# Causal stage of a four-block transformer kernel: gathering, inverting and fanning out the row sums of sixteen heads on four column groups

## What is computed

```python
dot = jnp.einsum('bhid,bhjd->bhij', q, k)                    # 16 heads of 16 features
vals = q_norm_sq + k_norm_sq.transpose(0, 1, 3, 2)
scores = dot * dot / (vals - 2.0 * dot + EPSILON)
scores = scores + mask[None, None, :, :]                     # causal
attn = jax.nn.softmax(scores, axis=-1)
out = jnp.einsum('bhij,bhjd->bhid', attn, v)
out = out.transpose(0, 2, 1, 3).reshape(b, t, e)
return out @ w_out + b_out
```

## Time and profile before

| | |
|---|---|
| median of 3 runs | 4438.76 us (4423.53 to 4446.45) |
| the profiled execution's own time | 4425.89 us |
| its span | 4423.8 us |
| PE, DVE, ACT, POOL busy | 93%, 75%, 57%, 38% |
| mean granted TensorE clock | 0.958 |
| causal stage alone, about | 2110 to 3070 us of the span |

### The profile page before, as it was taken

How to read it: one execution, slowest core, us unless ns; L and a number is a source line. 1 busy time by engine, 2 the same in 40 slices (tenths; PEclk the granted TensorE clock), 3 DMA queues, 4 the chain that set the end, 5 groups by cost and what they waited for, 6 DMA issues and landing times.

```text
span 4423.8 us, 65583 instructions
## 1 busy us (share of the span) xinstructions
PE 4125.5 (93%) x23120; PEld 2600.6 (59%) x23120; DVE 3305.6 (75%) x7689; ACT 2542.8 (57%) x5481; POOL 1674.1 (38%) x1816
## 2 busy tenths in 40 slices
PE   8999989999999999988888877888999999999998
PEld 5566556666666666555555555555566666666664
DVE  5767777777667767659899999988677777677663
ACT  4555554445444545449888998876454454454441
POOL 2222355546546546420001001013465464465441
PEclk9999999999999999997888998988999999999998
DMA  2000000000000000000000001101000000100000
GB/s 79 11 16 6 25 10 6 3 3 6 23 22 18 13 8 10 23 22 18 20 22 21 22 18 28 37 18 31 7 6 3 3 25 8 35 15 17 13 20 22
DMA packets 63062, 78.57 MB, mean 18 GB/s; under 512 B 15313, under 2 KB 47361, under 8 KB 62737
## 3 DMA queue, kind: packets, MB, share of 16 engines
q1 hardware_dynamic: 62736, 74.39, 5.9%
HBM read 36.63 MB, written 12.58 MB: 11 GB/s over the span
## 4 chain that ended last, share of the span: by engine, by line
PE 65%; DVE 21%; issue 6%; ACT 5%; POOL 2%; DMA 0%; SPq 0%; DVEq 0%; ACTq 0%; POOLq 0%
PE wide L863 45%; PE o_ps L863 8%; PE wide L866 6%; PE turn_ps L866 5%; DVE x L1291 2%; DVE turned L1342 2%; DVE w_up L1391 2%; DVE prob L1414 1%; PE turn_ps L863 1%; DVE prob L1403 1%; DVE w_up L1385 1%; DVE x L1397 1%; ACT prob L1247 1%; POOL prob L1607 1%; DVE hid L1397 1%
## 5 line engine op out<-in xcount | busy, mean ns | idle before, releaser
L863 PE MATMUL wide<-x,w_up 128*128 128x512 f32 (+3 forms) x2528 | 847.3, 548 | 4.2 <-DVE x L1494 2.4
L863 PE MATMUL wide<-w_in,x_t 128*128 128x512 f32 (+2 forms) x1920 | 813.1, 567 | 17.2 <-ACT q_t L1164 8.4
L1607 POOL TENSOR_SCALAR prob<-prob,st 128x256 f32<-128x256 f32 (+1 forms) x1024 | 501.2, 508 | 777.5 <-DVE st L1427 775.1
L1227 ACT ACTIVATE prob<-prob,st 128x256 f32<-128x256 f32 (+1 forms) x1024 | 479.4, 472 | 274.1 <-DVE st L1414 273.8
L863 PEld LDWEIGHTS wide<-w_in,x_t 128*128 128x128 f32 x1920 | 341.6, 192 | 368.9 <-issue 359.9
L863 PEld LDWEIGHTS wide<-x,w_up 128*128 128x128 f32 (+2 forms) x2528 | 370.9, 195 | 292.3 <-issue 270.2
L863 PE MATMUL o_ps<-pt,v 128*32 128x128 f32 (+2 forms) x5120 | 501.7, 341 | 18.8 <-DVE pt L1443 9.1
L1580 POOL TENSOR_TENSOR sines<-raw,rot 128x512 f32<-128x512 f32 x256 | 353.4, 1401 | 327.0 <-ACT raw L1152 326.9
L1588 POOL TENSOR_TENSOR rn<-ss,minus_half 128x16 f32<-128x16 f32 x128 | 424.3, 3315 | 105.4 <-DVE ss L1337 98.6
L863 PEld LDWEIGHTS o_ps<-pt,v 128*64 128x64 f32 (+1 forms) x5120 | 322.1, 131 | 235.4 <-issue 146.0
L1258 ACT ACTIVATE o_t<-o_ps 128x512 f32<-128x512 f32 x192 | 114.2, 595 | 484.0 <-PE o_ps L863 484.0
(11 more groups left out here) (161 smaller groups left out, 7481.6 us busy)
## 6 DMA issues: line engine op xcount, KB each, us to landing
kept<-resid SPq DMA_DIRECT2D x16, 512.0 KB, 2.7
x<-kept SPq DMA_DIRECT2D x16, 512.0 KB, 3.3
w_up<-hid SPq DMA_DIRECT2D x62, 128.0 KB, 2.2
x<-hid SPq DMA_DIRECT2D x62, 128.0 KB, 2.4
shifted<-resid SPq DMA_DIRECT2D x32, 224.0 KB
w_in<-in_f_wqkv SPq DMA_DIRECT2D x4, 1536.0 KB, 6.5
w_up<-in_f_w SPq DMA_DIRECT2D x4, 1492.0 KB, 6.7
resid<-in_x SPq DMA_DIRECT2D x8, 512.0 KB, 8.2
```

The costliest lines, as they stand in the source:

```text
L863: return eng.matmul(out, lhsT, rhs, start=start, stop=stop, skip_group_check=True)
L1227: last = eng.activation(pr[:, local_span(t)], pr[:, local_span(t)], ACT.Exp, bias=sm[:, t:t + 1], scale=-1.0, accum_out=sm[:, 4 + t:5 + t])
L1607: last = eng.tensor_scalar(pr[:, local_span(t)], pr[:, local_span(t)], sm[:, 8 + t:9 + t], 1.0, ALU.mult, ALU.mult)
```

## The change

In `sel` the four products no longer accumulate into the same 16 partitions. Each has 32 columns of weights (one matrix `sum_rows`, 128x32, for all) and writes its own 32 partitions, 32g to 32g+31, of `turn_ps`; a plane's four sums stand there eight times over. `olog` and `osum` work on 128 partitions of 512 where they worked on 16; `b_weight` and `o_rest` become 128 partitions high. Fan i reads its weights and its moving rows from partitions 32i to 32i+3: four rows, in another row group each time. The planner's duration for `sel` goes from 2.5 to 1.2 us. The two constants change shape (16 and 64 KB instead of 32 and 32 KB).

```diff
-            "bk": 0.65, "bq": 0.62, "proj": 1.72, "xt2": 1.0, "up_g": 3.55, "up_h": 3.55, "down": 2.85, "sel": 2.5, "fan": 0.62,
+            "bk": 0.65, "bq": 0.62, "proj": 1.72, "xt2": 1.0, "up_g": 3.55, "up_h": 3.55, "down": 2.85, "sel": 1.2, "fan": 0.62,
...
-        over4 = lambda a: a.rearrange("p (g n) -> p g n", g=GROUPS)
...
-        b_weight = shifted[0:BHEADS, :, :].rearrange("p t n -> p (t n)")
+        b_weight = shifted[:, :, :].rearrange("p t n -> p (t n)")
         b_down = w_down[:, :, :].rearrange("p c n -> p (c n)")
-        o_rest = b_down[0:BHEADS, 1024:1536]
-        sum_rows, sum_fan = over4(b_down[:, 0:4 * BHEADS]), over4(b_down[0:BHEADS, 512:1024])
+        o_rest = b_down[:, 1024:1536]
+        sum_rows, sum_fan = b_down[:, 0:BROW], b_down[:, 512:512 + P]
...
                     for g in range(GROUPS):
-                        last = mm(turn_ps[0:BHEADS, :], sum_rows[:, g, :], o_t[:, g, :], g == 0, g == GROUPS - 1)
+                        last = mm(turn_ps[BROW * g:BROW * (g + 1), :], sum_rows, o_t[:, g, :], True, True)
                     last.then_inc(S["sel"], 1)
                 elif kind == "fan":
                     pe.wait_ge(S["osum"], 2 * nth("osum", u))
-                    mm(turn_ps[:, :], sum_fan[:, i, :], b_weight, True, True).then_inc(S["fan"], 1)
+                    rows = slice(BROW * i, BROW * i + BHEADS // GROUPS)
+                    mm(turn_ps[:, :], sum_fan[rows, :], b_weight[rows, :], True, True).then_inc(S["fan"], 1)
...
-                    eng.activation(b_weight, turn_ps[0:BHEADS, :], ACT.Ln).then_inc(S["olog"], 1)
+                    eng.activation(b_weight, turn_ps[:, :], ACT.Ln).then_inc(S["olog"], 1)
...
-                    eng.tensor_tensor(o_rest, turn_ps[0:BHEADS, :], b_weight, ALU.mult).then_inc(S["osum"], 1)
+                    eng.tensor_tensor(o_rest, turn_ps[:, :], b_weight, ALU.mult).then_inc(S["osum"], 1)
...
-    sums, fan = np.zeros((GROUPS, P, BHEADS)), np.zeros((GROUPS, BHEADS, P))
-    for h in range(BHEADS):
-        first = BROW * (h % 4)
-        sums[h // 4, first + BHD, h] = 1.0
-        fan[h // 4, h, first:first + BHD] = -1.0
+    sums, fan = np.zeros((P, BROW)), np.zeros((P, P))
+    for m in range(BHEADS // GROUPS):
+        sums[BROW * m + BHD, m::BHEADS // GROUPS] = 1.0
+        for g in range(GROUPS):
+            fan[BROW * g + m, BROW * m:BROW * m + BHD] = -1.0
```

More of the change, by code:

```diff
@@ L1790, in constants @@
         "causal_floor": np.concatenate([np.full((P, 3 * P), DEN_MIN)] + 2 * [np.where(j > i, DEN_MAX, DEN_MIN)], axis=1), "causal_keep": np.where(i > j, 0.0, 1.0),
-        "sum_rows": sums.transpose(1, 0, 2), "sum_fan": fan.transpose(1, 0, 2),
+        "sum_rows": sums, "sum_fan": fan,
     }
```

## The result

The changed kernel took 4461.76 us (median of 6, 4459.10 to 4469.67), the kernel before 4435.59 us in the runs beside it (median of 6, 4423.14 to 4446.45). So the changed kernel is slower: the interval lies clear of 1, and holds the 0.5% that the prediction took for the least that can be told. The profiled executions took 4459.1 and 4425.9 us; the span after is 4456.9 us, its mean granted clock 0.946 where it was 0.958.

What follows compares the result with a forecast made beforehand. VectorE was taken to bound the causal stage, plus its waits while TensorE runs at 1.2 GHz. 4425.9 - 6.4 + 28 = 4447.5 us, plus 2.5, gave 4450 us; range for 8 in 10: 4420 to 4467 us.

Steps and rivals of the forecast that it cites:

- The four products: `sel` on TensorE: four column groups overlap, 3.61 us becomes 1.2 (1.1 to 2.0), gaining 2.4 us of TensorE per unit.
- Inversion on 128 partitions at no cost: ScalarE's Ln and VectorE's refinement take about as long on 128 partitions as on 16: 0.3 us in all, counted as zero.
- Nothing gained directly in units 25 to 29: Behind `sel` there, ScalarE and VectorE come straight from other work and reach the row sums when they did before: zero.
- Gains in units 24, 30 and 31 (6.4 us): The shorter `sel` cuts waiting behind it: 3.1 us in unit 24, 3.0 in unit 30, 0.3 in unit 31.
- The clock falls from the first fan to the middle of `proj`, VectorE idle 7.0 us in it: Units 26 to 29 do as unit 25 did: clock near 0.5 behind the gap, 7.0 us of VectorE time lost each.
- 28 us for four units: Clock loss in units 26 to 29 of the causal stage: 4 x 7.0 = +28 us, ends 0 and +28.
- The gap as the cause: Behind the shorter `sel`, TensorE idles 0.8 and 3.0 us instead of 1.48 ahead of the first fan, which lowers its clock.
- Fans from four rows at zero: Fan products last as their 512 columns do, whatever the rows: zero, bounds 0.1 us either way for each of 32.
- The order stays nearly as it is: With the planner's `sel` at 1.2 us, ScalarE's and VectorE's order hardly moves; one reordered unit could cost or give a few us.
- the clock holds: Rival, chance 0.28: the planner fills the gap behind `sel` and the clock falls no oftener; range 4412 to 4438 us.
- nothing overlaps: Rival, chance 0.07: `sel`'s four products run one behind the other, it stays 3.6 us; 4439 us.
- The slower one: Rival, chance 0.20: without the dense `sel` the clock stays low until `proj` in units 24 and 30 too; 4466 us.

Runs made afterwards that it cites:

- experiments 6: Changed kernel with the earlier kernel's order of work, plus three unused full-width products ahead of the first fan of units 25 to 29: 4452.11 us, ratio 1.0064.
- experiment 10: Changed kernel with the earlier kernel's order of work and fans of 128 rows, zero weights except in four: 4421.57 us, ratio 1.0003.
- experiment 5: Changed kernel with the earlier kernel's order of work and `sel`'s four products issued four times over (3.64 us): 4448.76 us, ratio 1.0055.
- experiment 1: Changed kernel with the planner's duration for `sel` put back to 2.5 us, so the earlier kernel's order of work: 4452.61 us, ratio 1.0076.
- Experiment 2: Kernel before with only the planner's duration for `sel` set to 1.2 us, so old products in the changed kernel's order: 4459.55 us, ratio 1.0087.
- experiment 9: Changed kernel with the earlier kernel's order, `sel`'s products issued four times over and fans of 16 rows, 12 with zero weights: 4428.32 us, ratio 1.0015.
- experiment 8: Changed kernel, earlier order, three unused products ahead of first fans in units 25 to 29, one ahead of each of 192 `bden`: 4451.98 us, ratio 1.0063.
- experiment 11: Changed kernel with the earlier kernel's order, `sel`'s products issued four times over and fans of 128 rows: 4414.22 us, ratio 0.9978.

## Why the prediction was right and wrong

The forecast was 0.25% above the kernel before, measured was a ratio of 1.0065. The range of 4420 to 4467 holds the 4461.76; of the three outcomes it is "slower by over 0.5%" (chance 0.22), by little (the interval begins at 0.44%), and not "the same" (0.65). Direction, place and engine were forecast; that the number stays within the range is in part luck, since two terms that the prediction put at nothing, the fans and the order, each turned out able to cost this much, and they did not add up. For the profiled execution the sum had -6.4 + 28 = +21.6 us, measured was +33.2: some 18 us more lost and 6.5 more won. Point by point:

- *The four products:* right. 1.07 us for 1.2 forecast, in eight records at full clock. The Trainium skill's sentence that a weight load overlaps running products only when it is for another row group (TensorE: Matmul & The Clock Gate, Part 3) does not fit here: the eight loads, all on every row group, were done within 0.16 us, while the first of the products ran, and the whole came out 3.4 times faster.
- *Inversion on 128 partitions at no cost:* right, a mean of 586 and 684 ns beside 0.59 and 0.67 us on 16.
- *Nothing gained directly in units 25 to 29:* right; ScalarE and VectorE had no idle time before they took the sums up.
- *Gains in units 24, 30 and 31 (6.4 us):* only partly borne out. From `sel` to `sel`, unit 24 won 3.8 us and unit 30 2.6; that these make 6.4 is chance, since unit 30 won them outside the stretch behind `sel`, unit 25 won 0.3 and the two ends of the stage 6.3 that no term had. The `sel` of unit 24 was also misread: 5.36 us is not 1.2 GHz throughout (eight records would take 7.1 at half speed), and the new one took 1.94 us, not 2.3. VectorE's wait behind `sel` went from 3.08 to 1.42 us in unit 24, and from 4.31 us to none in unit 30. From the trace of the changed kernel:

```profile
2101.80 0.69 DVE L1451 TENSOR_TENSOR w_down<-turn_ps,shifted 128x512 f32<-128x512 f32 x1 [1.42 <-ACT shifted L1267]
...
2948.57 0.69 DVE L1451 TENSOR_TENSOR w_down<-turn_ps,shifted 128x512 f32<-128x512 f32 x1
```

- *The clock falls from the first fan to the middle of `proj`, VectorE idle 7.0 us in it:* right as to place, engine and size. The stretch behind `sel` is 7.7 to 8.5 us longer in units 26 to 29, and in unit 26 VectorE is idle 5.3 us in the 14 and 2.60 before the residual sum.
- *28 us for four units:* mis-sized. They lost 46.0, and lasted 141 to 147 us where 136 to 138 were forecast. Of the 46.0, 32.4 us lie between `sel` and the residual sum; 13.6 lie in the rest of the units, which I had counted at nothing. Part of that is a further fall later in a unit. The window from 2451 on of the changed kernel, and the like one of before (the same 0.77 us of GpSimd and 28 GB/s in it):

```profile
2451.00:2461.00 10.00, 9.12 (x54) 6.04 (x54) 8.34 (x21) 8.71 (x16) 0.77 (x2) 0.50 0.12 28
```
```profile
2446.00:2456.00 10.00, 7.09 (x82) 4.88 (x78) 9.48 (x23) 9.15 (x16) 0.77 (x2) 1.00 0.12 28
```

  Counted in windows of 1 us from 2100 to 3090, the clock was under 0.75 in 253 of them before and in 365 after. How the 13.6 us divide between such falls and work moved by the order was not worked out further.
- *The gap as the cause:* the step that failed. Behind a longer gap the clock is down (experiments 6 and 10 show it before and in the first fan), but with fans of 128 rows it costs 3 us in a unit, not 7 (experiment 10), and undoing it leaves most of the loss while the fans have four rows (experiment 5). What it would cost with fans of 16 rows was not run. I had taken one unit that loses the clock as proof of what a gap does, and did not ask why the clock stays down for 14 us in which TensorE is never idle. The gap was misread too, as 0.8 and 3.0 us. The 0.8 came from taking the exponentials that end at 2378.62 for those that the six transposes behind `sel` wait for; they belong to the step after. In the changed kernel the transposes follow `sel` with no wait, and in the old order the gap is one, of 4.05 us (experiment 1).
- *Fans from four rows at zero:* the step that was costliest. The bounds of 0.1 us a fan were read off durations, and a product of few rows does last as its columns do (0.66 us at full clock in experiment 5). It cost through the clock of everything behind it: 1.0055 against 1.0015 between 4 and 16 rows, at one order, one `sel` and one gap (their intervals just meet), and 0.0074 between 4 and 128 rows in the changed kernel itself.
- *The order stays nearly as it is:* wrong. 233 of ScalarE's 2385 entries and 274 of VectorE's 3137 moved, and round `osum` the copying `pt_b` of step 1 now stands ahead of it, which the prediction had named as a sign of being wrong. Experiment 2 lost 0.87% by the order alone, with the clock low behind its fans. With fans of 128 rows the same order cost nothing, so its price hangs on the narrow fans. Which of its moves costs wasn't tested.
- *The rivals.* That the clock holds, and that nothing overlaps, both fell. The slower one gave 4466 us and its mechanism was there: the stretch behind `sel` grew by 3.1 us in unit 30, though `sel` was 4.2 us shorter, and in unit 24 shrank by 0.9 us with a `sel` 3.4 us shorter. From `sel` to `sel` both units still won, so it isn't what made the time. Unit 30 behind `sel`, the changed kernel first, then before:

```profile
2954.00:2975.00 21.00, 20.57 (x95) 13.96 (x95) 15.57 (x33) 12.42 (x24) 0.00 (x0) 0.67 0.06 13
```
```profile
2913.00:2933.00 20.00, 19.83 (x112) 12.77 (x110) 18.79 (x43) 13.00 (x24) 0.00 (x0) 0.91 0.06 14
```

Left open: whether a fan of 128 rows helps by its height alone or also because it can no longer run beside `bden`, as fans of 4 and 16 rows do (experiment 9 shows height at work without that, from 4 to 16); whether 16 rows would be enough with the short `sel`; and, since each kernel was traced in one execution, how often each unit loses the clock.

## What to carry to other kernels

Where TensorE is busy but not the bound, ask of every changed product not only how long it lasts but what it does to the granted clock of the stretch in which the bounding engine waits: cutting a weight matrix to the few rows that count saves no time and can cost the clock, while padding it with zero rows lasts no longer and here kept the clock or brought it back sooner. Read the windows' clock, not the kernel's mean, and read it beside what TensorE was doing. A duration changed in a planner is an edit of its own and wants a run of its own.

## What the runs showed of the hardware

- TensorE busy for all of 14 us stayed at 0.52 of its clock, so at 1.2 GHz nearly throughout, in fans of 4 rows, products of 16 and 18 rows, 128x128 transposes and mixing. With fans of 128 rows it was back at 1.00 within 8 us, behind a gap of 4.05 us (experiment 10). The Trainium skill (TensorE: Matmul & The Clock Gate, Part 1) tells of low clocks behind idle gaps and during warm-up, and that activity lifts them; that the height of the fans makes a difference as well I had not expected, and these runs show it. The rows added had zero weights, with inverses moving past them.
- Four products on four column groups, all of them on every row, ran in 1.06 to 1.07 us at a clock of 1.00 where one behind the other they took 3.61.
- The highest mean clock of all, 0.979, went with 4451.98 us (experiment 8), and the fastest kernel's, 4414.22 us, was the 0.958 of the kernel before (experiment 11).
